# A mixture-of-experts layer on one core: partial sums and biases seeded in PSUM, another product order, reloads moved

## The reference

```
logits = xf @ gate_w.T;  topv, topi = top_k(softmax(logits), 2)
disp[slot of (token, expert)] = rotated token
h   = relu(disp @ fc1_w.T + fc1_b)     # per expert: 1024 x 512 @ 512 x 2048
eo  = h @ fc2_w + fc2_b                # per expert: 1024 x 2048 @ 2048 x 512
out = x + sum over the two experts of gate * eo[slot]
```

## Time and profile before

| | |
|---|---|
| median of three executions | 1593.59 us |
| profiled execution | 1585.56 us, of it 1583.8 us span |
| TensorE busy | 1410.8 us, 89% |
| VectorE busy | 1180.5 us, 75% |
| ScalarE busy | 681.5 us, 43% |
| GpSimd busy | 373.3 us, 24% |
| granted clock, mean | 0.961 |

### The profile page before, as it was taken

How to read it: one execution, slowest core, us unless ns; L and a number is a source line. 1 busy time by engine, 2 the same in 40 slices (tenths; PEclk the granted TensorE clock), 3 DMA queues, 4 the chain that set the end, 5 groups by cost and what they waited for, 6 DMA issues and landing times.

```text
span 1583.8 us, 18277 instructions
## 1 busy us (share of the span) xinstructions
PE 1410.8 (89%) x6090; PEld 1130.0 (71%) x6090; DVE 1180.5 (75%) x1928; ACT 681.5 (43%) x1072; POOL 373.3 (24%) x294
## 2 busy tenths in 40 slices
PE   8537999899998998989988999999989999999997
PEld 5325777677776776767776777787768777778885
DVE  6786788687795778767786877887788777876653
ACT  5224444344452443533443444544445444544442
POOL 1050002540044200640016400242005400350022
PEclk9657999999999999999999999999999999999999
DMA  8453554565545644465454655456546555454232
GB/s 305 162 123 73 114 120 100 141 159 114 112 120 144 142 108 94 126 175 116 102 112 140 154 122 106 119 176 130 112 95 179 143 125 110 118 148 86 53 100 85
DMA packets 455727, 200.46 MB, mean 127 GB/s; under 512 B 398816, under 2 KB 401001, under 8 KB 453714
## 3 DMA queue, kind: packets, MB, share of 16 engines
q1 hardware_dynamic: 437538, 146.95, 40.0%
q0 software_dynamic: 18096, 52.35, 11.2%
HBM read 159.50 MB, written 39.98 MB: 126 GB/s over the span
## 4 chain that ended last, share of the span: by engine, by line
PE 30%; DVE 23%; issue 13%; SPq 13%; POOL 8%; DMA 8%; ACT 6%; another core or an unknown queue 0%; ACTq 0%; DVEq 0%; POOLq 0%
SPq L221 12%; DVE yfull L747 5%; PE ps L993 5%; PE ps L994 5%; PE ps L998 5%; DVE w1t L683 5%; DMA x_blk<-slots_dram 4%; PE ps L965 4%; PE ps L967 3%; PE ps L966 3%; POOL out L369 3%; POOL rows L358 3%; ACT yfull L455 2%; DVE w_lo L705 2%; POOL gate_now L361 1%
## 5 line engine op out<-in xcount | busy, mean ns | idle before, releaser
L965 PE MATMUL ps<-yc_hi,w1c_hi 128*128 128x512 f32 x896 | 357.5, 399 | 77.1 <-DVE h L853 20.7
L993 PE MATMUL ps<-w_hi,h_hi 128*128 128x512 f32 x960 | 381.7, 398 | 43.5 <-DVE w_lo L705 43.5
L994 PE MATMUL ps<-w_lo,h_hi 128*128 128x512 f32 x960 | 379.7, 396 | 0.0
L966 PE MATMUL ps<-yc_lo,w1c_hi 128*128 128x512 f32 x896 | 351.0, 392 | 0.0
L967 PE MATMUL ps<-yc_hi,w1c_lo 128*128 128x512 f32 x896 | 350.9, 392 | 0.0
L965 PEld LDWEIGHTS ps<-yc_hi,w1c_hi 128*128 128x128 f32 x896 | 169.4, 189 | 135.5 <-ACT s L497 28.4
L369 POOL DMA_INDIRECT out<-rows,scatter_row x64 | 131.2, 2051 | 568.7 <-DVE rows L778 555.9
L998 PE MATMUL ps<-w_hi,h_lo 128*128 128x512 f32 x960 | 259.8, 393 | 0.0
L436 ACT ACTIVATE w_hi<-w_raw 128x512 fp32r<-128x512 f32 x256 | 159.9, 625 | 215.6 <-PE ps L998 130.7
L993 PEld LDWEIGHTS ps<-w_hi,h_hi 128*128 128x128 f32 x960 | 183.4, 191 | 89.7 <-DVE w_lo L705 51.3
L705 DVE TENSOR_TENSOR w_lo<-w_raw,w_hi 128x512 fp32r<-128x512 f32 x256 | 175.7, 686 | 55.2 <-ACT w_hi L436 55.0
(11 more groups left out here) (157 smaller groups left out, 1491.6 us busy)
## 6 DMA issues: line engine op xcount, KB each, us to landing
w_raw<-in_L_ffn_fc_w SPq DMA_DIRECT2D x256, 256.0 KB
w_raw<-in_L_ffn_fc_w SPq DMA_DIRECT2D x512, 64.0 KB
slots_dram<-x_blk SPq DMA_DIRECT2D x28, 512.0 KB, 3.8
x_blk<-slots_dram SPq DMA_DIRECT2D x224, 64.0 KB
out<-x_all SPq DMA_DIRECT2D x8, 1024.0 KB, 13.1
x_all<-in_x SPq DMA_DIRECT2D x7, 1024.0 KB, 13.6
b_bc<-in_L_ffn_fc_b POOLq DMA_DIRECT2D x8, 256.0 KB
x_all<-in_x SPq DMA_DIRECT2D x4, 256.0 KB, 4.7
```

The lines of the kernel that those rows point to most:

```text
L965: pe.matmul(bank, hi, yc_hi[:, y, q, :], start=first and q == 0, stop=False, skip_group_check=True)
L966: pe.matmul(bank, hi, yc_lo[:, y, q, :], start=False, stop=False, skip_group_check=True)
L993: pe.matmul(eo_s[:, b, :], h_hi[:, c, blk], w2_hi[:, w, :], start=(tile == 0), stop=False)
L994: pe.matmul(eo_s[:, b, :], h_hi[:, c, blk], w2_lo[:, w, :], start=False, stop=False)
```

## The change

ScalarE's copy of p1 to `s1` and VectorE's c11 addition give way to a seed: ScalarE writes p1 + b1 into bank 1 (`seed_c11`), and TensorE adds p2 onto it. Likewise b2 is written by ScalarE into the four banks of `eo` (`seed_eo`) before fc2 adds to them, and `add_b2` goes. `set_bits` runs a matmul on each bank once at the start, so that later matmuls add to what stands there. The products come in the order p6, p2, fc2, p7, p5, p1 of the next group, p4, p3, fc2; expert by expert, p1 of groups 0 and 1 come first. Rotations are 512 columns wide, on four turned blocks. Slab 1's rows have their own place, four tiles of `h1` that are free by then. The store of x is issued by GpSimd right behind its gather; units are turned in groups 0, 1, 4 and 5, and SyncE's cuts are placed accordingly. The gates of an expert are gathered together and ahead.

```diff
-    B11, B21, T2, T1, T3, B22, T4 = range(7)
+    B11, B21, T2, T3, T1, T4, B22 = range(7)
+        slab_rows = (rows[:, :, :], h1[:, ROWS1:ROWS1 + SB, :])      # ROWS1 = 4
...
 SyncE:
+            cut_x(0)
             for e in range(E):
                 for g in range(GROUPS):
-                    if not last and g in (2, 4, 6): store_x(4 * e + g // 2)
+                    if not last and g == 2:
+                        cut_x(4 * e + 2)
+                    if e < E - 2 and g == 6:
+                        cut_x(4 * e + 4)
                     load_w2(N + 3)
                     load_w2(N + 4)
                     if G + 3 < E * GROUPS:
                         load_w1(G + 3)
-                    if not last and g in (2, 4, 6): cut_x(4 * e + g // 2)
+                    if not last and g == 0:
+                        cut_x(4 * e + 1)
+                    if not last and g == 4:
+                        cut_x(4 * e + 3)
-                    if e < E - 2 and k == 8: store_x(4 * (e + 1))
-                    if e < E - 2 and k == 11: cut_x(4 * (e + 1))
 GpSimd:
             def gather_x(V):
...
+                for bb in range(2):
+                    pool.wait_ge(blk_in[bb], 16 * (V + 1))
+                pool.dma_start(slots_dram[V % 2].rearrange("b p d -> p b d"), x_blk[:, :, :]).then_inc(cut_out, 16)
+            def load_b2(e):
+                if e:
+                    pool.wait_ge(eo_seeded, 2 * SB * e)
+                pool.dma_start(b2_bc[:, :], b2_rows[e:e + 1, :].partition_broadcast(P)).then_inc(b2_in, 16)
...
             for e in range(E):
-                    for u in range(1, 4): gather_x(4 * e + u)
+                    gather_x(4 * e + 1)
+                    gather_x(4 * e + 2)
+                    gather_gates(e + 1)
+                    gather_x(4 * e + 3)
+                    if e < E - 2:
+                        gather_x(4 * e + 4)
                 scatter_rows(2 * e)
+                if not last:
+                    load_b2(e + 1)
+                pool.wait_ge(h_ready, e * STEPS + HT + ROWS1 + SB)
                 gather_rows(2 * e + 1)
-                if e < E - 2: gather_x(4 * (e + 1))
                 scatter_rows(2 * e + 1)
                 if not last:
                     gather_rows(2 * e + 2)
 ScalarE:
+            def seed_c11(G):
...
+                act.activation(ps[:, BANK_C11, :], running(G), ACT.Identity, bias=b1T[:, e * HT + 2 * g:e * HT + 2 * g + 1]
+                               ).then_inc(c11_seeded, 1)
+            def seed_eo(s, b):
+                act.wait_ge(b2_in, 16 * (s // 2 + 1))
+                act.activation(ps[:, EO[s % 2] + b, :], b2_bc[:, :], ACT.Copy).then_inc(eo_seeded, 1)
...
                     act.activation(s3[:, :], running(G), ACT.Relu, bias=odd_bias).then_inc(c21_kept, 1)
                     if G + 2 < E * GROUPS:
                         w1_high(G + 2)
+                    if not last and g == 1:
+                        first_of_slab(e + 1, 0)
+                    if not last and g == 5:
+                        first_of_slab(e + 1, 1)
...
+                        if tile >= HT - SB:
+                            b = tile - (HT - SB)
+                            act.wait_ge(sums_ready, SB * 2 * e + b + 1)
+                            seed_eo(2 * e + 2, b)
 VectorE, in a group:
                     dve.wait_ge(p2_done, G + 1)
-                    dve.scalar_tensor_tensor(s1[:, :], ps[:, BANK_P2, :], b1_now[:, 2 * g:2 * g + 1], s1[:, :], ...)
-                    w1_low(G + 1)
+                    low_of(N, ps[:, BANK_C11, :])
                     w2_low(N)
-                    if not last and g % 2 == 1:
-                        turn_x(4 * e + g // 2)
+                    if not last:
+                        if g < 2:
+                            turn_x(4 * e + g)
+                        elif g < 5:
+                            rotate(e + 1, 0, g - 1)
+                        elif g == 5:
+                            turn_x(4 * e + 3)
+                        else:
+                            rotate(e + 1, 1, g - 5)
                     dve.wait_ge(p5_done, G + 1)
                     dve.wait_ge(s3_ready, G + 1)
                     dve.scalar_tensor_tensor(h1[:, 2 * g + 1, :], ps[:, BANK_P5, :], bias[1], s3[:, :], ...)  # c22_done
                     w2_low(N + 1)
+                    if not last and g == 4:
+                        turn_x(4 * e + 2)
                     turn_w1(G + 2), sum_w1(G + 2, 0 to 2)
                     dve.wait_ge(p3_done, G + 1)
                     dve.scalar_tensor_tensor(h1[:, 2 * g, :], ps[:, BANK_P5, :], bias[0], s2[:, :], ...)      # c12_done
+                    h_lo(N + 1)
+                    w1_low(G + 2)
 TensorE, in a group:
+                    product(S2, T2, par, bank, False, False, p6_done)
+                    p2(G)                            # product(A12, B21, ..., ps[:, BANK_C11, :], False, True, p2_done)
+                    fc2(N - 2)
+                    product(S3, T3, par, bank, False, False, p7_done)
+                    product(S1, T1, par, ps[:, BANK_P5, :], True, False, p5_done)
+                    p1(G + 1)                        # for 1 <= g < GROUPS - 1
                     product(A22, T4, par, bank, False, True, p4_done)
                     pe.wait_ge(c22_done, G + 1)
                     product(S4, B22, par, ps[:, BANK_P5, :], False, True, p3_done)
                     fc2(N - 1)
```

More of the change, by code:

```diff
@@ L292, in _ @@
                         load_w1(G + 3)
[L293 to L296, removed]
+                    if not last and g == 0:
+                        cut_x(4 * e + 1)
+                    if not last and g == 4:
+                        cut_x(4 * e + 3)
+                for tile in range(HT):
+                    N = e * STEPS + HT + tile
                     if N + 3 < E * STEPS:
                         load_w2(N + 3)
[L299 to L302, removed]
         @block.gpsimd
@@ L444, in y_high, with first_term @@
                 act.activation(yc_hi[:, slot, :, :], src, ACT.Copy).then_inc(yc_hi_ready, 1)
-            def take_b1(e):
-                if e:
-                    act.wait_ge(c12_done, GROUPS * e)
+            y11, y12 = yfull[:, 0:2, 0:SLAB], yfull[:, 0:2, SLAB:2 * SLAB]
+            y21, y22 = yfull[:, 2:4, 0:SLAB], yfull[:, 2:4, SLAB:2 * SLAB]
+            def first_term(src, to):
+                for i in range(Q):
+                    act.activation(to(i), src, ACT.Copy, scale=rot[:, i, 0:1]).then_inc(y0_done, 1)
@@ L542, in _ @@
                     await_step(act, N - 4)
-                    act.activation(h_hi[:, N % 4, :], h1[:, N % HT, :], ACT.Relu).then_inc(h_hi_ready, 1)
+                    act.activation(h_hi[:, N % 4, :], h1[:, tile, :], ACT.Relu).then_inc(h_hi_ready, 1)
                     w2_high(N)
@@ L795, in _ @@
                                      ).then_inc(tables_ready, 1)
+            w1_low(0)
             turn_w1(1)
@@ new lines, in _ @@
+                    w2_low(N)
+                    if not last:
[5 more added lines that the diff above has]
+                            turn_x(4 * e + 3)
+                        else:
+                            rotate(e + 1, 1, g - 5)
+                    if e and 2 * g == ROWS1:
+                        dve.wait_ge(rows_out, 16 * SB * 2 * e)
@@ L859, in _ @@
-                if not last:
-                    rotate(4 * e + 3, 3)
-                for k in range(-2, HT - 2):
-                    N = e * STEPS + HT + 2 + k
-                    low_of(N, h1[:, N % HT, :])
+                        w1_low(G + 2)
+                for tile in range(HT):
+                    N = e * STEPS + HT + tile
+                    low_of(N, h1[:, tile, :])
                     w2_low(N)
-                    if k == 0:
+                    if tile == 2:
                         add_rows(2 * e)
@@ L997, in fc2, with set_bits, p1 @@
                     blk = slice(b * P, (b + 1) * P)
-                    ins = pe.matmul(eo_s[:, b, :], h_lo[:, c, blk], w2_hi[:, w, :], start=False, stop=False)
+                    ins = pe.matmul(eo_s[:, b, :], h_lo[:, c, blk], w2_hi[:, w, :], start=False, stop=False, skip_group_check=True)
                 ins.then_inc(fc2_step, 1)
-            def p1(e, g):
-                G = e * GROUPS + g
+            def set_bits(banks):
+                for bank in banks:
+                    ins = pe.matmul(ps[:, bank, :], w1c_hi[:, 0, A11, 0:P], yc_hi[:, B11, 0, :], start=True, stop=True)
+                ins.then_inc(bits_set, 1)
+            def p1(G):
+                e, g = G // GROUPS, G % GROUPS
                 if g == 0:
```

340 lines of the change are left out of this document (161 added, 179 removed).

## The result

In 20 runs each on the same chip the changed kernel took 1589.93 us (median; 1583.1 to 1596.15), the kernel before 1582.91 (1569.99 to 1599.36). The ratio is 1.0054, with a 95% interval of 1.0031 to 1.0077: slower by half a per cent. Every ratio in this document leaves out the executions of a kernel that were over 1.5% above its fastest on that chip, which for the widely spread kernel before can be most of them, so a ratio can differ from that of the medians.

A forecast was written before the change was run, and what follows sets the result against it. TensorE, 89% busy, was taken as the bound, losing time to long stalls and short waits. 1585.6 - 16 (six experts) - 7.5 (expert 0) - 3.5 (end) = 1559 us, range 1500 to 1600.

The forecast's parts named there:

- Part 1: Product order and seeds: TensorE's short waits for s2 (18.6 us), even (20.7) and odd h tile (14.3) all go.
- Part 2: Store moved from SyncE to GpSimd: four long TensorE stalls on w2's low part, some 10 us each, go; 40 us.
- Part 3: Reload of the single x buffer becomes a new TensorE wait; six experts take 1084 us against 1100.
- The loop: Turn, gather, store, cut, turn of the one x buffer takes 16.2 us, with 3.5 for the gather's landing.
- Group 1: TensorE comes to p3 at about B + 22.0 (B: expert's first product) and waits 9.5 us for the odd h tile.
- Group 5: From group 4 to 5 TensorE waits 3.6 us, 29.4 against 25.8.
- The clock: Slow matmuls at 1.2 GHz after a stop cost 2.4 us behind group 1's wait, 1.2 behind group 5's.
- Part 4: Both ends of the kernel: 7.5 us less in expert 0, 3.5 less behind 1358.62.
- The reload is no stop: Rival, 22%: loop pieces overlap or VectorE arrives later, so the 16.7 us per expert mostly disappear: 1449 us.
- GpSimd becomes the bound: Rival, 12%: a second 10 us scatter hold makes b2 and ScalarE's seeds late, starving fc2 in slab 1: 1614 us.
- One cancels the other: Rival, 6%: short waits stay because VectorE, released late in groups 1 and 5, passes its lateness on: 1587 us.
- The rule against the store on GpSimd: Skill rule: VectorE can lock out GpSimd's descriptor writes; the sum keeps 3.8 us per store, 9 us would give 1622.

The follow-up runs named there:

- experiment 7: Kernel before, with GpSimd's x gather for the next but one expert's first unit moved ahead of slab 0's scatter: 1573.13 us, ratio 0.9951.
- experiment 8: Kernel before, with slab 1's four add_b2 moved from its last tiles to behind the last tile's low parts: 1590.08 us, ratio 1.0103.
- experiment 9: Kernel before, with both the x gather ahead of slab 0's scatter and slab 1's add_b2 behind the last tile: 1546.23 us, ratio 0.984.
- experiment 2: Changed kernel with a second x buffer for odd units, in two free tiles of h1: 1451.38 us, ratio 0.9269 to the kernel before.
- experiment 5: Changed kernel with the store of x issued by SyncE again, directly ahead of its cuts: 1584.36 us, ratio 1.0069 to the kernel before.

## Why the prediction was wrong, by its own steps

The mechanism that it named is the one that decided: the reload loop took the place of the short waits, with TensorE stopped for the odd h tile at groups 1 and 5. Its sign came too: VectorE's turn waited 12.2 to 13.7 us at group 1 in six experts (about 14 forecast) and 8.0 to 8.9 at group 5. But the forecast was 27 us faster, and the result 7 us slower (1.1 by the profiled executions, 28 us from the sum). The time was a difference of two sums of about 120 us. Before, six experts lost 1100.1 - 6 x 163.3 = 120 us; after, 6 x 21.2 = 127, where I had 6 x 17.4 = 104. An error of a fifth in the second turned the sign.

**Part 1 (short waits, product order, seeds): right.** Three of the four rows went; the fourth, the odd h tile, grew by the reload of part 3. The unknown prices came out near what was taken: ScalarE's write into PSUM with a bias 662 ns (0.68 taken), and 512-wide rotations 2.73 us for four, 0.68 each (0.68 taken).

```profile
L489 ACT ACTIVATE ps<-ps,b1T 128x512 f32<-128x512 f32 x64 | 42.3, 662 | 152.9 <-PE ps L1004 128.5 <-remote 21.2 <-issue 3.2
```

**Part 2 (four long stalls): right in size, half right in cause.** They went. But I put them on SyncE's `store_x` alone; experiments 7 to 9 show that the change had to remove both routes, and it did, since `add_b2` went too.

**Part 3 (the reload): the step that failed, by the size of its terms.** By rows of the expert shown above (B = 671.2):

- *The loop.* 17.6 us in place of 16.2. The cuts to the turn took 7.3, as taken, and the store to the cuts 3.2 (3.9). The x gathers took 5.55 us from the second one's issue to the store, in place of 3.5, and 6.6 in the loop of group 1. This is the link that was mis-sized. The median landing of x gathers is 4.7 us now, where the earlier trace rows has 3.5; experiment 2, without any stop, has 5.0 for the units in `x_blk`. What stands beside the late landings, in stretches from a second gather's issue to its landing before, and to the store after:

```profile
1254.17:1257.77 3.60, 3.60 (x18) 2.98 (x17) 3.14 (x8) 1.87 (x3) 1.02 (x1) 1.00 0.52 148
```

```profile
684.44:691.06 6.62, 6.62 (x31) 5.49 (x30) 4.15 (x5) 4.13 (x6) 0.95 (x2) 1.00 1.12 209
752.39:757.94 5.55, 5.55 (x26) 4.60 (x25) 4.50 (x7) 2.43 (x3) 0.95 (x2) 1.00 0.98 173
```

  The last two numbers are the DMA engines' busy share (a packet counts whole where it starts, so it can pass 1) and GB/s: the gathers after land in a stretch that is twice as full by the share. SyncE issues the eight cuts of w1 there (681.95 to 688.55 and 751.49 to 757.63). I counted the cuts of w1 issued between an x gather's issue and its landing, from 200 us on: in the trace before none for 49 of 50 gathers, in the trace after 3 to 6 for each of the 48. In experiment 2, 34 gathers have 3 to 6, with a median landing of 4.7 us, and 12 have none, with 3.8. So the new order laid two loads on each other that the earlier trace rows had met apart. This is read from the traces; no run moved w1's cuts, so the cause is not shown by experiment.
- *Group 1.* GpSimd came to the x gather at B + 11.9 (13.5 forecast), TensorE wanted p3 at B + 22.0 (22.0). The start was earlier and the loop longer: p3 ran at B + 33.0 where I had 31.5. The mean wait of six experts is 10.7 us, start to start, in place of 9.5.
- *Group 5.* 4.7 us on average in place of 3.6.
- *The clock.* I priced it at 2.4 us behind the long stop and 1.2 behind the short one, as if the short one lay between a free wait and a dear one. It is not so graded: here 1.7 behind 10.80 us and 2.5 behind 4.49. Clock and small things together are 5.9 us per expert in place of 4.3.

Per expert these are 1.2 + 1.1 + 1.6, with rounding 3.8 us more (21.2 - 17.4), 23 in six: the difference between -16 and +6.8. The two ends bring the other 5 of the 28.

**Part 4 (both ends): half right.** p3 of group 1 in expert 0 ran at 148.88 (148.0 forecast). Group 5 of that expert then waited 6.3 us and lost its clock, where 4.8 for both had been put: 2.8 us gained in place of 7.5. Behind 1358.62, 2.9 in place of 3.5.

**The rivals.** *The reload is no stop* was wrong for this kernel, but its price, 1449, is what the change is worth without the loop: 1451 (experiment 2). *GpSimd becomes the bound* did not come: it had one scatter of 7.2 to 7.7 us and one gather of 5.0 to 6.8 in each of seven experts, and TensorE waited for neither. *One cancels the other* named nearly the right total (1587) by luck, for a wrong reason: the short waits did not stay.

**The rule against the store on GpSimd** moved nothing (experiment 5); the 3.8 us kept in the sum were 3.2.

## What to carry to other kernels

A wait with a loop behind it (turn, gather, store, load, turn) belongs behind the work that feeds the busiest engine, or needs a second buffer; on an in-order engine the place of two turns per expert was worth 127 us of 1590. When a change takes one sum of waits away and brings another as large, forecast the two apart, and price the links of the new loop by what the new order puts beside them: a gather that landed in 3.5 us with the DMA engines half busy took 4.5 to 6.6 in these loops, beside w1's cuts. Before one wait is called the cause of a stall, look for a second one behind the same late data: with either alone removed the stalls stayed.

## What the hardware showed that I had not expected

**What a stop costs in clock hardly depends on its length, once it is long.** I counted TensorE's idles between 250 and 1400 us, from one matmul's start to the next less 0.2268, in the traces of all twelve kernels, and looked whether matmuls at half the rate followed:

| idle, us | how many | followed by 6 to 14 half-rate matmuls |
|---|---|---|
| 1.0 to 1.9 | 140 | 0 |
| 1.95 to 2.03 | 31 | 5 |
| 2.7 to 3.3 | 5 | 4 |
| 3.9 to 16 | 67 | 67 |

Behind those of 3.9 us and more 1.5 to 3.0 us are lost, and no more behind the long ones: 12 matmuls behind 4.7 us, 8 behind 10.4, 12 behind 15.6. The idles of 2.7 to 3.3 us are those of the third way in experiment 9 (four, all followed) and one in experiment 7 (not followed). These are counts of this case, too few between 1.9 and 3.9 us to say more. Most of part 1's waits, of up to 1.7 us in the profile's count, were therefore cheap, and each of the new stops was dear.

**GpSimd's long instructions recur.** One scatter of slab 0's rows took 10.0 us in five experts of the trace before, and one took 7.2 to 7.7 in seven experts of the one after, where most take 1.0 to 1.4. A gather of rows behind it took 7.2 to 7.6 us in four of the five, and 5.0 to 6.8 in all seven. Three of the scatters after:

```profile
266.00 7.68 POOL L376 DMA_INDIRECT out<-rows,scatter_row  x1 [0.30 <-issue]
450.26 7.69 POOL L376 DMA_INDIRECT out<-rows,scatter_row  x1 [0.30 <-issue]
634.01 7.70 POOL L376 DMA_INDIRECT out<-rows,scatter_row  x1 [0.30 <-issue]
```

How many experts have one varies between variants of the kernel before (five in it, seven in that of experiment 8), and that kernel's runs spread from 1555 to 1599 us. In experiment 2 the long instructions come in seven experts too, but TensorE waits for none of them, and its four runs spread by 1.2 us. The store of x is not what holds them: with it on SyncE (experiment 5) the scatters take the same 7.7 us in seven experts. What does was not tried.
